# Max products of a grouped-query attention placed by a table of their own: about one a step, up to four units ahead

## The reference

```python
y = x * rsqrt(mean(x * x) + 1e-6) * rms_w
q, k, v = split(y @ w_in.T)                # 32 query heads, 8 key/value groups, 64 wide
q, k = rope(q), rope(k)
qk = where(causal, q @ k.T * 64 ** -0.5, -inf)
o = softmax(qk) @ v                        # four query heads share the k and v of a group
x = x + x_in + o @ w_out.T                 # x_in: the normalised input
h = silu(x_n @ Wu.T) * (x_n @ Wg.T)        # Wu, Wg, Wd rounded to -1, 0, 1 times a scale
x = x + x_n + h @ Wd.T
```

## Time and profile before

| | |
|---|---|
| median of three runs | 2225.39 us |
| profiled execution | 2226.72 us |
| its span | 2224.9 us |
| attention, first to last exponential | 100 to 1664 us |
| group 3 (a group without the branch) | 692.31 to 883.44 us, 191.1 us |
| group 2 (begins at the branch) | 491.47 to 692.31 us, 200.8 us |
| PE busy | 91% of the span |
| DVE, POOL, ACT busy | 70%, 61%, 45% |

### The profile page before, as it was taken

One profiled execution on the slowest core, in us unless ns is written; L12 is line 12 of the kernel. 1 busy time (PEld: TensorE's weight loads), 2 busy tenths in 40 slices (PEclk: granted clock), 3 DMA queues, 4 the chain that ended last, 5 costly groups with the idle time before them and its releaser, 6 DMA issues. The chain is left out here.

```text
span 2224.9 us, 61534 instructions
## 1 busy us (share of the span) xinstructions
PE 2015.6 (91%) x22015; PEld 1226.3 (55%) x22015; DVE 1549.4 (70%) x2914; ACT 998.9 (45%) x2281; POOL 1348.4 (61%) x1470
## 2 busy tenths in 40 slices
PE   2589999988999999899999889999987988999998
PEld 1356665665666566566656656665663443444443
DVE  8479878967986896798689679868963774222221
ACT  3245655554565555456555545655552111211210
POOL 5467777776777777677777767777770442311311
PEclk9999999999999999999999999999998999999999
DMA  5432233223223322322332232233216540000000
GB/s 174 139 51 46 40 68 69 44 43 70 47 43 68 59 44 52 73 48 40 68 59 43 53 71 47 43 68 61 43 38 224 199 162 36 1 19 19 0 19 19
DMA packets 307602, 139.78 MB, mean 63 GB/s; under 512 B 253664, under 2 KB 291296, under 8 KB 305760
## 3 DMA queue, kind: packets, MB, share of 16 engines
q1 hardware_dynamic: 307296, 135.79, 26.8%
HBM read 50.53 MB, written 25.17 MB: 34 GB/s over the span
## 5 line engine op out<-in xcount | busy, mean ns | idle before, releaser
L833 POOL TENSOR_TENSOR pl<-p 128x512 f16<-128x512 f32 (+3 forms) x801 | 759.3, 961 | 182.0 <-ACT p L667 179.1
L762 DVE TENSOR_REDUCE mpart<-a_ps 128x1 f32<-128x512 f32 (+3 forms) x1288 | 717.2, 596 | 154.2 <-PE a_ps L581 84.5
L667 ACT ACTIVATE p<-a_ps 128x512 f32<-128x512 f32 (+3 forms) x1283 | 660.1, 531 | 333.2 <-PE a_ps L596 183.7
L612 PE MATMUL a_ps<-v,p 128*128 128x65 f16 x4352 | 531.4, 193 | 38.7 <-POOL pl L833 22.1
L614 PE MATMUL a_ps<-v,p 128*128 128x64 f16 x4352 | 532.1, 195 | 0.0
L616 PE MATMUL a_ps<-v,pl 128*128 128x65 f16 x4352 | 528.6, 193 | 0.0
L612 PEld LDWEIGHTS a_ps<-v,p 128*128 128x128 bf16 x4352 | 410.4, 97 | 163.8 <-DVE pl L754 33.6
L578 PE MATMUL a_ps<-k_hl,q_hh 128*128 128x512 f16 (+3 forms) x1288 | 445.7, 350 | 54.6 <-issue 23.2
L754 DVE TENSOR_TENSOR pl<-p 128x512 f16<-128x512 f32 (+2 forms) x482 | 449.2, 935 | 30.1 <-ACT p L667 30.1
L595 PE MATMUL a_ps<-q_hh,k_hl 128*128 128x512 f16 (+3 forms) x1283 | 447.7, 349 | 18.4 <-DMA q_lm<-qk_lo 18.4
L614 PEld LDWEIGHTS a_ps<-v,p 128*128 128x128 bf16 x4352 | 407.6, 98 | 81.7 <-issue 0.7
(11 more groups left out here) (98 smaller groups left out, 2708.0 us busy)
## 6 DMA issues: line engine op xcount, KB each, us to landing
attn_scratch<-o_turn SPq DMA_DIRECT2D x64, 256.0 KB, 3.0
p_att<-attn_scratch SPq DMA_DIRECT2D x32, 512.0 KB, 4.4
raw<-ffn_t SPq DMA_DIRECT2D x12, 1024.0 KB, 4.9
wraw<-w_in_t SPq DMA_DIRECT2D x9, 768.0 KB, 6.0
resid_scratch<-xin SPq DMA_DIRECT2D x4, 1024.0 KB, 4.3
raw<-w_out_t SPq DMA_DIRECT2D x1, 4096.0 KB, 15.0
x<-resid_scratch SPq DMA_DIRECT2D x4, 1024.0 KB, 8.0
out<-x SPq DMA_DIRECT2D x16, 256.0 KB, 2.0
```

The lines of the kernel that those rows point to most:

```text
L612: nc.tensor.matmul(o, weights, v[:, par, j, 0:VU], start=(j == 0 and t == 0), stop=False, skip_group_check=True)
L667: nc.scalar.activation(p32[:, i % RING, r * P:CHUNK], sbank(i)[:, r * P:CHUNK], ACT.Exp, scale=SCALE).then_inc(exp_done, 1)
L762: nc.vector.reduce_max(mpart[:, u % 2, t, kk:kk + 1], side_bank(part, ("piece", ahead, u, i))[:, 0:width], AX.X)\
L833: nc.gpsimd.tensor_tensor(pl[:, i % RING, cols], p32[:, i % RING, cols], p_high[:, i % RING, cols], ALU.subtract).then_inc(low_pool, 1)
```

## The change

Every max product gets a place in a table, `PIECE_SLOTS`, by chunk: chunk 1 (units 4 to 7) over steps 0 to 31, chunk 2 over 32 to 71, chunk 3 over 72 to 131, chunk 0 of the next group over 132 to 159, spread evenly in each. The four projections of each chunk get other steps. Their number, the steps and every instruction of a step stay as they are.

| steps | max products before | now | projections before | now |
|---|---|---|---|---|
| 0 to 7 | 8 | 8 | none | 4 |
| 8 to 15 | 16 | 8 | 8, 11, 15 | 8, 12 |
| 16 to 31 | 16 | 16 | 18 | 16 |
| 32 to 47 | 24 | 20 | 36, 41, 47 | 34, 40, 46 |
| 48 to 71 | 24 | 28 | 53 | 52 |
| 72 to 95 | 32 | 26 | 74, 83, 93 | 78, 87 |
| 96 to 131 | 33 | 38 | 102, 128 | 97, 106 |
| 132 to 159 | 7 | 16 | 133, 138, 143 | 134, 137, 141, 144 |

In `OPENING` units 2 and 3 of group 0 now have their 8 max products too, and SP transposes `q_lm` of unit 2 there. In `transfers()` the time at which `q_hh` of a unit is wanted follows from its first max product.

```diff
+PIECE_SLOTS = {(0, 1): (0, 32), (0, 2): (32, 72), (0, 3): (72, 132), (1, 0): (132, STEPS)}
...
-    out += [(None, None, [(0, 1, i)]) for i in range(KEY_TILES[1])]
+    out += [(None, None, [(0, u, i)]) for u in range(1, HG) for i in range(KEY_TILES[u])]
...
-    place(range(first[2], first[5] - 2), 0, 2)
-    place(range(first[6] + 4, first[9] - 1), 0, 3)
-    place(range(first[10] + 2, first[13]), 1, 0)
-    place(range(first[14], first[15] + 4), 1, 1)
...
-            pieces = [(ahead, w, i) for i in range(m) if i * n // m == j]
+    place(range(4, 20), 0, 2)
+    place(range(34, 58), 0, 3)
+    place(range(78, 116), 1, 0)
+    place(range(134, 148), 1, 1)
+    pieces = {n: [] for n in range(STEPS)}
+    for (ahead, c), (begin, end) in PIECE_SLOTS.items():
+        chunk = [(ahead, u, i) for u in range(HG * c, HG * (c + 1)) for i in range(KEY_TILES[u])]
+        for n, piece in enumerate(chunk):
+            pieces[begin + n * (end - begin) // len(chunk)].append(piece)
...
-            wanted = UNITS * ahead + HG * c + h - 2
-            wanted = STEPS * (wanted // UNITS) + FIRST_STEP[wanted % UNITS]
+            wanted = next(STEPS * (ahead - a) + m for m, (_, _, pieces) in enumerate(SLOTS)
+                          for a, u, i in pieces if u == HG * c + h and i == 0)
```

More of the change, by code:

```diff
@@ L286, in place @@
             jobs[slots[t * len(slots) // TPC]] = ("proj", ahead, TPC * c + t)
-    first = FIRST_STEP
-    place(range(first[2], first[5] - 2), 0, 2)
-    place(range(first[6] + 4, first[9] - 1), 0, 3)
-    place(range(first[10] + 2, first[13]), 1, 0)
-    place(range(first[14], first[15] + 4), 1, 1)
[L293 to L298, removed]
-            pieces = [(ahead, w, i) for i in range(m) if i * n // m == j]
-            out.append((FIRST_STEP[u] + j, jobs.get(FIRST_STEP[u] + j), pieces))
+    place(range(4, 20), 0, 2)
[7 more added lines that the diff above has]
+            pieces[begin + n * (end - begin) // len(chunk)].append(piece)
+    out = [(n, jobs.get(n), pieces[n]) for n in range(STEPS)]
     return out
@@ L513, in _ @@
             query_low(0, 0, 1, 0)
+            for h in range(2, HG):
+                if ("lm", 0, h, 1) in TRANSFERS:
+                    query_low(0, 0, h, 0)
             keys(0, 1, 0, 0)
@@ L553, in take_bank @@
                     elif part is SLOTS:
-                        side_read("piece", 0, 1, KEY_TILES[1] - 1)
+                        side_read("piece", 0, HG - 1, KEY_TILES[HG - 1] - 1)
                     return side_bank(part, item)
```

## The result

The changed kernel takes **2212.90 us** (median of four runs, 2209.97 to 2213.69), the kernel before 2225.71 in the same session (2225.27 to 2226.97, four runs). The ratio is 0.9939 with a 95% interval of 0.9922 to 0.9956. That is 12.8 us less, where 44 were forecast: the sign is right and the time lies inside the range, but the gain is less than a third of the forecast.

A forecast was written before the change was run, and what follows sets the result against it. PE, busy 91% of the span, was taken as the bound; only its stops could go. Per group 4.7 + 4.1 - 1.6 + 1.45 - 3.1 = 5.55 us, times eight 44.4: 2181 us, 8-in-10 range 2144 to 2214.

The forecast's parts named there:

- the terms of the forecast: PE's forecast work in one group's six stretches: steps 0 to 31, 32 to 47, 48 to 71, 72 to 95, 96 to 131, 132 to 159.
- the gain counted for the branch groups: Groups beginning at the branch (200.8 us) were given the same gain as the others, 5.55 us each.
- 28.0, a loss of 1.6: Steps 48 to 71, 26.4 us before: four more max products make DVE the bound; loss 0.5 to 2.5 us.
- 34.1, a loss of 3.1: Steps 132 to 159, 31.0 us before: nine more max products, one more projection, same POOL wait; loss 1.7 to 4.5.
- 35.9, a gain of 4.7: Steps 0 to 31, 40.6 us before: `q_lm` and bank stops go, POOL is late next; gain 3.2 to 6.7.
- The 2.5 us left for a stop behind POOL: Steps 0 to 31: PE time still lost as POOL's lows wait behind the reciprocal, bounded 0.5 to 4 us.
- I take the two as equal: Opening: 1.2 to 4 us extra against group 0's 4.1 us further gain at `q_lm`; bounds 4 us either way.
- DVE takes over: Rival, steps 48 to 131: DVE lows grow from 1.00 to 1.15; gain 2.6 us a group, 2206 us, chance 0.12.
- POOL takes over: Rival, head and tail: 4 us bound in steps 0 to 31, 35.5 in 132 to 159; 2205 us, chance 0.12.
- slower, DVE and POOL block each other: Rival, steps 48 to 131: DVE lows average 1.45 us; group 1.5 us longer than before, 2237 us, chance 0.09.

The follow-up runs named there:

- the products alone: Changed kernel with the projections back in their old steps, so only the max products moved against the kernel before: 2213.93 us, ratio 0.9947 to the kernel before.

## Why the prediction was wrong in size

**The mechanism of the gain held.** The waits for `q_lm` and for the keys are gone. One part of it was not as told: the `q_lm` stop was put down to the max products alone, and the moved projections take it away by themselves. Steps 32 to 47 took 20.9 us (21.3 forecast), steps 72 to 131 66.5 (66.2). PE's own work and the prices of products and projections were right: the six stretches, each less its stops by starts, add up to 176.5 us where the terms of the forecast had 176.6 (33.4, 20.5, 24.9, 27.0, 38.4 and 32.4).

**The steps that failed are the three in which I sized what is late next, and the gain counted for the branch groups.** Over the attention 44.4 us were forecast, the opening at nothing; 22.7 less 4.2 for the opening came, 25.9 fewer. Of these the four ordinary groups have 11.3, the other four and the opening 14.6. In ordinary groups the sum forecast 185.6 us; it was 188.8. Of the 3.3 us missing, steps 48 to 71 have 1.7, the tail 0.9, the head 0.8, and steps 72 to 131 0.3; 0.4 came back in steps 32 to 47. (Group 5 misses only 1.5, for the reason under the branch groups.)

- *Steps 48 to 71* ("28.0, a loss of 1.6"): 29.7. DVE's work was forecast at 27.8 and was 28.2. I set DVE's sum against the length of the whole stretch, as if its free time anywhere in it could be used. It can't: DVE was idle for 1.5 us in steps 48 to 59, then had 15.21 of 15.25 us filled in steps 60 to 71, where all four splits of the weights stand. Two experiments show it from two sides: moving two lows to POOL took 3.2 us off steps 60 to 71, spreading the splits 0.85.
- *Steps 132 to 159* ("34.1, a loss of 3.1"): 35.0. PE's wait for POOL lows, which I took over unchanged at 1.8 by starts, became 2.1, with 0.5 more in stops too short to be named, since POOL has a fourth projection among its lows. Two lows moved to DVE took 1.3 us off.
- *Steps 0 to 31* ("35.9, a gain of 4.7"): 36.7. The 2.5 us left for a stop behind POOL were spent otherwise: 1.3 by starts for a POOL low, 1.1 for an exponential, 0.8 for a reduction in steps 4 to 7. I had blamed the first on the reciprocal behind a projection. POOL's wait for reciprocals fell from 11.2 to 4.3 us, and POOL worked without a gap for the 13 us up to the low of step 25. Moving two lows off it took the stop away, so the amount of its work made this low late. Whether the wait of 3.6 us that ended 18 us before had a part in it is open.

**The branch groups.** I counted the full gain for them. Groups 4 and 6 gained 0.1 and 0.7 us. In group 4 steps 0 to 7, in which PE starts again after the branch, grew from 13.9 to 15.5 us, with one projection there that was not before, and the rest gained 1.7. Beside group 3, group 4 misses 0.7 us there and 1.5 in steps 32 to 47, group 6 0.2 and 1.5: in both, steps 32 to 47 had less to lose before (24.7 us against 25.4, the stop for the keys 1.2 us against 1.9) and take 21.6 instead of 20.9 now. Group 2 gained 5.0 and group 0 6.0, and group 5, an ordinary one, 4.0: in these three the stop for the keys, 2.0 to 2.5 us long, was followed in the kernel before by a granted clock of 0.50 (steps 32 to 47: 27.2, 27.6 and 27.1 us, mean clock 0.94). I read group 3 alone, where that didn't happen.

**The opening.** "I take the two as equal" held by the sum: it cost 4.2 us, and group 0 gained 3.7 more than group 3.

**The rivals.** "DVE takes over" and "POOL takes over" had the right time (2206, 2205) and each was half right: the middle is DVE's, the tail POOL's, and both happened, with a gain of 2.3 us in three of the four ordinary groups against the 2.6 and 2.7 that I gave them singly. I priced them as alternatives with 0.12 each, where one does not exclude the other, and so the middle of the forecast was too low. The mechanism that I gave the first was wrong: DVE's lows didn't lengthen. All of 512 columns between 500 and 1500 us, DVE's, then POOL's (columns: busy us, mean ns, idle before them):

```profile
L757 DVE TENSOR_TENSOR pl<-p 128x512 f16<-128x512 f32 x227 | 218.0, 960 | 13.6 <-ACT p L670 13.6
...
L836 POOL TENSOR_TENSOR pl<-p 128x512 f16<-128x512 f32 x349 | 397.4, 1149 | 78.7 <-ACT p L670 77.9
```

960 ns against 1003, and in steps 48 to 131 of group 3 979 against 1054. With that the case "slower, DVE and POOL block each other" has no ground either. By the Trainium skill ("SBUF — State Buffer", "Who interferes with whom") a reduction never contends with GpSimd. The trace agrees: a reduction of 512 columns takes 678 ns before and 679 after, the longest of any width 693 in both. (The rows ahead of the prediction give only their means and not this narrow spread.)

**Where the forecast gain went.** Each half of the change removed its stops, one of them the same, and each paid part of it back to the same lows. With those moved, the change brings 20 us over the kernel before with the same lows; with the queries earlier too, some 38. That is near the 44 of the forecast, but of another pair of kernels, and the earlier queries were not tried in the kernel before.

## What to carry to other kernels

When a schedule is evened out on one engine, sum the work of every other engine over short stretches and not over a phase: here 12 steps showed the bound that 24 hid. That the lag behind PE, five steps here, sets how far off free time can be used is argued and not tried. Rivals that name different stretches can all happen, so add their prices rather than give each a chance of its own. And let the same change rebalance the work that follows the moved one (here six of 160 lows between DVE and POOL and three steps of lead for a transfer), because PE reaches every transfer earlier afterwards. Read more than one repetition, too: the stop for the keys cost 1.2 to 2.5 us by the group, and in three of eight a slow clock came on top.

## What was not expected of the hardware

A stop of 2.3 us of PE inside a busy stretch was followed by about 3 us at a granted clock of 0.50 (1.2 GHz), so that it cost 3.4 us and not 2.3. The length of the stop doesn't tell whether this happens. In the kernel with the products alone PE stood 2.3 us for the keys in group 0, and the clock stayed at 1.00 (2.4 GHz) through steps 32 to 47; in group 5 it stood 2.0 us, and the clock fell. Steps 32 to 47 of group 0, the same of group 5, and the 4.5 us behind its stop:

```profile
146.83:170.89 24.06, 21.08 (x265) 13.87 (x262) 18.64 (x37) 11.88 (x31) 16.21 (x22) 1.00 0.36 73
1104.80:1130.15 25.35, 22.70 (x264) 14.71 (x261) 18.89 (x37) 11.87 (x31) 16.22 (x22) 0.93 0.34 70
1107.50:1112.00 4.50, 4.50 (x44) 2.80 (x44) 2.18 (x4) 1.19 (x2) 1.99 (x3) 0.62 0.69 159
```

The same transposing transfer of `q_hh` at the same place, directly behind a store of 256 KB, landed after 3.0 to 3.2 us in six groups of an execution and after 4.6 and 4.7 in two, with no cause that the traces show.
